# A four-layer cross-attention kernel on one core: the ternary feed-forward stage joined and re-staged, and an opening that waits for two batches only

## The reference

```python
def bitlinear(x, W, b):
    w_scale = jnp.clip(jnp.mean(jnp.abs(W)), EPS, None)
    Wq = _ste(W, jnp.clip(jnp.round(W / w_scale), -1.0, 1.0) * w_scale)
    x_scale = jnp.clip(jnp.max(jnp.abs(x), axis=-1, keepdims=True), EPS, None)
    xq = _ste(x, jnp.clip(jnp.round(x * (QB / x_scale)), -QB - 1.0, QB) * (x_scale / QB))
    return jnp.einsum('bnd,hd->bnh', xq, Wq) + b
h = bitlinear(x, W1, b1)          # 128 -> 512
h = jax.nn.gelu(h, approximate=False)
return bitlinear(h, W2, b2)       # 512 -> 128
```

## Time and profile before

| | |
|---|---|
| time, median of 3 runs | 2486.17 us (2484.84 to 2491.94) |
| the profiled execution: time | 2488.64 us |
| the profiled execution: span of its records | 2486.9 us |
| busy: PE, DVE, ACT, POOL | 2136.2, 1824.4, 1335.7, 1247.5 us |
| mean granted clock of PE | 0.946 of 2.4 GHz |
| opening, to the first record of the attention | 0 to 22.78 us |
| ternary phase, from its first record to the end | 2360.99 to 2486.9 us |

### The profile page before, as it was taken

One profiled execution on the slowest core, in us unless ns is written; L12 is line 12 of the kernel. 1 busy time (PEld: TensorE's weight loads), 2 busy tenths in 40 slices (PEclk: granted clock), 3 DMA queues, 4 the chain that ended last, 5 costly groups with the idle time before them and its releaser, 6 DMA issues. The chain is left out here.

```text
span 2486.9 us, 67321 instructions
## 1 busy us (share of the span) xinstructions
PE 2136.2 (86%) x22352; PEld 1629.6 (66%) x22352; DVE 1824.4 (73%) x4650; ACT 1335.7 (54%) x2821; POOL 1247.5 (50%) x1940
## 2 busy tenths in 40 slices
PE   5878997999988779599999997899789999998755
PEld 4557995556656568466666666666567888875523
DVE  5975554666659766489999968688698866667887
ACT  2444552444434456355555547355468888873466
POOL 4547635555535366477777745333264343334333
PEclk9978998999999879799999999899999999999978
DMA  8022211000000223200000000000000312210000
GB/s 307 20 112 76 78 53 30 16 13 14 11 2 1 83 76 105 62 13 11 9 9 11 8 2 21 10 1 0 19 5 2 103 56 67 56 43 15 1 11 24
DMA packets 82031, 96.69 MB, mean 39 GB/s; under 512 B 16720, under 2 KB 61136, under 8 KB 79760
## 3 DMA queue, kind: packets, MB, share of 16 engines
q1 hardware_dynamic: 73616, 77.12, 9.9%
q0 software_dynamic: 8192, 16.79, 2.3%
HBM read 56.51 MB, written 37.36 MB: 38 GB/s over the span
## 5 line engine op out<-in xcount | busy, mean ns | idle before, releaser
L1722 DVE TENSOR_TENSOR l2f_h_lo<-l2f_h,l2f_h_hi 128x512 fp32r<-128x512 f32 x256 | 187.1, 763 | 101.1 <-ACT l2f_h_hi L1643 101.0
L1012 POOL TENSOR_TENSOR a_pm<-a_pt,tri_post 128x256 f32<-128x256 f32 x256 | 179.6, 731 | 71.8 <-ACT a_pt L668 71.4
L1650 ACT ACTIVATE l2f_h<-l2f_f,ahead 128x512 f32<-128x512 f32 x256 | 174.2, 688 | 49.6 <-DVE l2f_h_lo L1722 32.5
L808 DVE TENSOR_REDUCE l1s_negm<-l1s_s 128x6 bf16<-128x768 f32 x128 | 123.1, 961 | 95.7 <-PE l1s_s L485 95.5
L1817 POOL TENSOR_TENSOR l2f_acc<-l2f_tmp,l2f_acc 128x512 f32<-128x512 f32 x56 | 73.0, 1303 | 207.2 <-DVE l2f_tmp L1740 207.2
L668 ACT ACTIVATE l1s_pt<-l1s_st 128x768 f32<-128x768 f32 x128 | 96.9, 812 | 144.9 <-PE l1s_st L523 144.9
L808 DVE TENSOR_REDUCE a_negm<-a_s 128x4 bf16<-128x1024 f32 x128 | 156.2, 1220 | 23.2 <-PE a_s L485 23.1
L1643 ACT ACTIVATE l2f_h_hi<-l2f_h 128x512 fp32r<-128x512 f32 x256 | 154.4, 633 | 0.0
L668 ACT ACTIVATE a_pt<-a_st 128x1024 f32<-128x1024 f32 x128 | 126.6, 1066 | 3.3 <-PE a_st L523 3.3
L684 ACT ACTIVATE a_q_hi<-a_pa 128x256 bf16<-128x256 f32 x64 | 24.5, 383 | 184.7 <-PE a_pa L451 184.7
L1534 PE MATMUL l2f_f<-l2f_x_hi,l2f_w_hi 128*128 128x512 f32 x256 | 101.7, 397 | 1.2 <-POOL l2f_w_lo L1804 1.2
(11 more groups left out here) (575 smaller groups left out, 6930.1 us busy)
## 6 DMA issues: line engine op xcount, KB each, us to landing
expert_rows<-zeros SPq DMA_DIRECT2D x16, 1056.0 KB, 17.5
l2f_wrow<-weights_by_expert SPq DMA_DIRECT2D x64, 256.0 KB, 3.2
l0f_w<-in_l0f_w SPq DMA_DIRECT2D x8, 640.0 KB, 9.7
l0f_x_in_sb<-expert_rows SPq DMA_DIRECT2D x72, 64.0 KB
expert_rows<-l0f_y SPq DMA_DIRECT2D x72, 64.0 KB, 1.6
l1f_x_in_sb<-expert_rows SPq DMA_DIRECT2D x72, 64.0 KB
expert_rows<-l1f_y SPq DMA_DIRECT2D x72, 64.0 KB
ahead<-in_l2f_w SPq DMA_DIRECT2D x6, 512.0 KB, 4.6
```

Source lines behind the costliest of these rows:

```text
L808: dve.tensor_reduce(dst, src, AX.X, ALU.max, negate=True).then_inc(max_done, 1)
L1012: last = pool.tensor_tensor(pm[:, par, heads_, kt, :], pt[:, par, heads_, kt * (T + P):kt * (T + P) + P], K["tri_post"][:].unsqueeze(1).br ...
L1650: act.activation(h[:, j], psum_f[j][:], ACT.Gelu, bias=col(e, j)).then_inc(h_ready, 1)
L1722: dve.tensor_tensor(h_lo[:, pos % 2, j], h[:, j], h_hi[:, pos % 2, j].bitcast(F32), ALU.subtract)\
```

## The change

**In the opening**, x is loaded in two parts, batches 0 and 1 ahead and the other 14 after the first weights; the end of the phase waits for the first part alone, and DVE waits for the rest (`arrived`) where the attention takes the statistics of batch 2. DVE clears `context_t`, `context_n` and `zeros` before it needs `begin_rstd`, and POOL makes `begin_rstd` after 10 of its 25 masks. ACT runs a one-element activation early.

The diff, cut to its core (line numbers of the changed kernel are some 5 to 35 higher):

```diff
-            sp.dma_start(x[:], a["x"].rearrange("b (t p) d -> p (b t) d", p=P)).then_inc(in_loaded, 16)
+            rows = a["x"].rearrange("b (t p) d -> p (b t) d", p=P)
+            first = slice(0, 2 * TT)
+            rest = slice(2 * TT, NT)
+            sp.dma_start(x[:, first, :], rows[:, first, :]).then_inc(in_loaded, 16)
             sp.dma_start(ctx_t[0:CK, :], a["ctx_t"]).then_inc(in_loaded, 16)
             fetch(sp, K, None, after)
+            sp.dma_start(x[:, rest, :], rows[:, rest, :]).then_inc(K["arrived"], 16)
...
-            dve.wait_ge(step, MASK_STEPS)
-            dve.tensor_reduce(K["own_slot"][:], K["slots4_8"][:].rearrange("p (u q) -> p u q", u=4), AX.X, ALU.add)\
-                .then_inc(filled, 1)
-            dve.wait_ge(filled, 2)
-            dve.wait_ge(rstd_ready, 1)
-            for t in range(CTILES):
-                last = dve.tensor_scalar(cn[:, t, :], c[:, t, :], mv[:, t, 0:1], rstd[:, t:t + 1],
-                                         ALU.subtract, ALU.mult)
-            last.then_inc(cn_ready, 1)
             dve.memset(ctx_t[CK:P, :], 0.0).then_inc(zeroed, 1)
             dve.memset(ctx_n[CK:P, :], 0.0)
             dve.wait_ge(zeroed, 1)
             dve.memset(ctx_t[CK:CK + 1, :], 1.0).then_inc(zeroed, 1)
             dve.memset(zeros[:], 0.0).then_inc(zeroed, 1)
             dve.wait_ge(zeroed, 3)
+            dve.wait_ge(rstd_ready, 1)
+            for t in range(CTILES):
+                last = dve.tensor_scalar(cn[:, t, :], c[:, t, :], mv[:, t, 0:1], rstd[:, t:t + 1],
+                                         ALU.subtract, ALU.mult)
+            last.then_inc(cn_ready, 1)
+            dve.wait_ge(step, MASK_STEPS)
+            dve.tensor_reduce(K["own_slot"][:], K["slots4_8"][:].rearrange("p (u q) -> p u q", u=4), AX.X, ALU.add)\
+                .then_inc(filled, 1)
+            dve.wait_ge(filled, 2)
...
+            pool.wait_ge(stats, 1)
+            pool.tensor_scalar(veps[:], mv[:, :, 1], EPS, None, ALU.add).then_inc(veps_ready, 1)
+            pool.wait_ge(veps_ready, 1)
+            pool.tensor_tensor(rstd[:], veps[:], K["half"][:, 0:CTILES], ALU.pow).then_inc(rstd_ready, 1)
...
+            act.activation(warm[:], g[:], ACT.Identity)
...
+                if clear and isinstance(b, int) and b == 2:
+                    dve.wait_ge(K["arrived"], 16)
...
-                if j == -4 and after_first is not None:
-                    after_first()
+                if j + 4 < len(between):
+                    between[j + 4]()
...
-                link(dve.tensor_scalar(wq[:], ws[:], 1.0 / QB, None, ALU.mult))
                 for i in range(2):
-                    link(dve.tensor_scalar(wf[i][:], wf[i][:], wr[:, i:i + 1], ROUND, ALU.mult, ALU.add))
-                    link(dve.tensor_scalar(wf[i][:], wf[i][:], ROUND, 1.0, ALU.subtract, ALU.min))
-                    link(dve.tensor_scalar(wt[i][:], wf[i][:], -1.0, None, ALU.max))
+                    link(dve.tensor_scalar(wq_by_part[:, i:i + 1], ws[:, 1 - i:2 - i], 1.0 / QB, None, ALU.mult))
+
+            def ternary(i):
+                link(dve.tensor_scalar(wf[i][:], wf[i][:], wr[:, i:i + 1], ROUND, ALU.mult, ALU.add))
+                link(dve.tensor_scalar(wf[i][:], wf[i][:], ROUND, 1.0, ALU.subtract, ALU.min))
+                link(dve.tensor_scalar(wt[i][:], wf[i][:], -1.0, None, ALU.max))
+
+            def first_weights():
+                ternary(0)
                 link(dve.tensor_scalar(b1w[:], b1b[:], wr[:, 0:1], QB, ALU.mult, ALU.mult))
                 dve.sem_inc(w_ready, 1)
...
+            def second_weights():
+                ternary(1)
+                dve.sem_inc(w_ready, 1)
+            def rounded(n, pn, q, pq):
+
+                has_h, has_x = inside(n), inside(q)
+                part = slice(0 if has_h else 1, 2 if has_x else 1)
+                if has_h:
+                    dve.wait_ge(h_ready, G * n + G)
+                    dve.tensor_reduce(most[:, 0, :], h[:, pn % 2], AX.X, ALU.max, apply_absolute_value=True)\
+                       .then_inc(qstep, 1 if has_x else 2)
+                if has_x:
+                    dve.wait_ge(xn_ready, q + 1)
+                    dve.tensor_reduce(most[:, 1, :], xn[:, pq % 2], AX.X, ALU.max, apply_absolute_value=True)\
+                       .then_inc(qstep, 1 if has_h else 2)
+                dve.wait_ge(qstep, QS * q + 2)
+                dve.tensor_scalar(clipped[:, part], most[:, part], EPS, None, ALU.max).then_inc(qstep, 1)
+                dve.wait_ge(qstep, QS * q + 3)
+                wait(dve, diag_ready, q - 1 if has_x else N)
+                dve.reciprocal(inverse[:, pq % 2, part], clipped[:, part]).then_inc(qstep, 1)
+                dve.wait_ge(qstep, QS * q + 4)
+                dve.tensor_scalar(scaling[:, part], inverse[:, pq % 2, part], QB, None, ALU.mult).then_inc(qstep, 1)
+                dve.wait_ge(qstep, QS * q + 5)
+                if has_h:
+                    wait(dve, hq_ready, n)
+                    for t in range(G):
+                        last = dve.tensor_scalar(hi[:, t], h[:, pn % 2, t], scaling[:, 0, t:t + 1], ROUND, ALU.mult, ALU.add)
+                    last.then_inc(hi_ready, 1)
+                if has_x:
+                    wait(dve, xq_ready, q)
+                    for t in range(G):
+                        last = dve.tensor_scalar(xi[:, t], xn[:, pq % 2, t], scaling[:, 1, t:t + 1], ROUND, ALU.mult, ALU.add)
+                    last.then_inc(xi_ready, 1)
+                    wait(dve, h_ready, G * (q - 3))
+                if has_h:
+                    wait(dve, o1_ready, n - 3)
+                rows = part.stop - part.start
+                dve.tensor_tensor(back[:, pq, part], clipped[:, part],
+                                  wq_by_part[:, part].unsqueeze(2).broadcast_to([P, rows, G]), ALU.mult).then_inc(qstep, 1)
...
                     dve.wait_ge(stats, k + 1)
                     dve.sem_inc(K["passed"], 1)
+                n, pn = at(0)
+                q, pq = at(3)
+                if inside(n) or inside(q):
+                    rounded(n, pn, q, pq)
...
+            run(dve, emit, (weight_sums, first_weights, second_weights))
...
         def _(pool):
             def emit(at):
-                q, pq = at(3)
-                if inside(q):
-                    pool.wait_ge(xstep, XS * q + 3)
-                    wait(pool, h_done, G * (q - 3))
-                    pool.sem_inc(K["passed"], 1)
-                    o = [P, G, P]
-                    pool.tensor_tensor(diag[:, pq], K["ident"][:].unsqueeze(1).broadcast_to(o),
-                                       xr[:, pq % 2, :].unsqueeze(2).broadcast_to(o), ALU.mult).then_inc(diag_ready, 1)
                 k, pk = at(4)
                 if inside(k):
                     pool.wait_ge(stats, k + 1)
                     wait(pool, xn_ready, k - 1)
+                    wait(pool, shift_ready, k)
...
-            pe.wait_ge(w_ready, 1)
...
+                    pe.wait_ge(hq_ready, l + 1)
+                    wait(pe, hq_t_ready, l)
                     for t in range(G):
                         for f in range(FB):
+                            last = pe.transpose(psum_t[:, t, f, :], hq[:, t, f * P:(f + 1) * P], K["ident_bf"][:])
+                    last.then_inc(h_turned, 1)
...
+                    pe.wait_ge(hq_t_ready, l + 1)
+                    if isinstance(l, int) and l == 0:
+                        pe.wait_ge(w_ready, 2)
+                    wait(pe, o1_ready, l)
...
+            act.activation(warm[:], K["half"][:, 0:1], ACT.Gelu)
...
-                        act.activation(h[:, pm % 2, t], psum_h[pm % 2][t][:], ACT.Gelu, scale=xd[:, pm, t:t + 1])\
+                        act.activation(h[:, pm % 2, t], psum_h[pm % 2][t][:], ACT.Gelu, scale=back[:, pm, 1, t:t + 1])\
                            .then_inc(h_ready, 1)
+                l, pl = at(-1)
+                if inside(l):
+                    act.wait_ge(h_turned, l + 1)
+                    wait(act, o_done, l - 1)
+                    act.activation(hq_t[:, pl % 2], psum_t[:], ACT.Identity).then_inc(hq_t_ready, 1)
                 n, pn = at(2)
...
+                n, pn = at(0)
+                if inside(n):
+                    act.wait_ge(hi_ready, n + 1)
+                    wait(act, h_turned, n)
+                    act.activation(hq[:], hi[:], ACT.Identity, bias=unround[:]).then_inc(hq_ready, 1)
+                q, pq = at(3)
+                if inside(q):
+                    act.wait_ge(xi_ready, q + 1)
+                    wait(act, x_turned, q - 1)
+                    act.activation(xq[:, pq % 2], xi[:], ACT.Identity, bias=unround[:]).then_inc(xq_ready, 1)
```

119 lines of the change are left out of this document (36 added, 83 removed).

## The result

The changed kernel takes 2462.77 us (median of 4 runs, 2459.79 to 2467.61) against 2486.62 us for the kernel before in the same comparison: ratio 0.9902, 95% interval 0.988 to 0.9925. I had forecast 2471 us, with 2464 to 2478 as the range. The two profiled executions are further apart, 27.1 us in span (2486.9 and 2459.8).

| stretch | before, us | after, us | less | forecast |
|---|---|---|---|---|
| up to the ternary phase | 2360.99 | 2353.31 | 7.7 | 4.3 |
| its lead-in, to the first reduction of h | 19.80 | 17.27 | 2.5 | } 4.3 |
| reductions 0 to 2 | 14.28 | 10.26 | 4.0 | |
| reductions 2 to 12 (ten steps) | 66.55 | 54.53 | 12.0 | 5.6 |
| from reduction 12 to the end | 25.28 | 24.43 | 0.85 | 0.8 |

What follows compares the result with a forecast made beforehand. DVE was taken to bound the steady ternary steps, chains across engines the lead-in, DVE's chain the opening. Opening 4.3, lead-in with first steps 4.3, ten steps 5.6 and end 0.8 sum to 15.0 us: 2471 us, range 2464 to 2478.

Steps and rivals of the forecast that it cites:

- three small instructions: Steady ternary step on DVE: three small instructions go, at 0.20 us each.
- clip: Steady step on DVE: `l3f_hc` no longer meets POOL's sum and takes 0.17 instead of 0.62 us, a gain of 0.45.
- collision moved: Steady step: POOL's 0.61 us diagonal slows the product or codes of h instead of `l3f_xi`; net 0.
- the loop's register work: Steady step: the hardware loop's register work is not hidden, so 6.1 us was taken instead of 6.02.
- None takes over: Steady step: neither ACT (4.8 us a step) nor PE (4.0) becomes the bound in place of DVE.
- the later turns: Steady step: the handover from h's codes through ACT and PE to the second layer is spread over two steps.
- Rival (b): Ternary steps: PE's two waits at its lower clock make 7.5 us a step, total 2489 to 2490; chance 0.04.
- Rival (a): Steady step: PE's new round trip sets 6.6 us, so the steady part gives nothing; total 2477, chance 0.17.
- the root first: Lead-in: POOL does the root ahead of the 0.61 us diagonal; part of the lead-in's and first steps' 4.3 us.
- the weights in parts: Lead-in: the second and third part of the weights (2.0 and 1.45 us) stand in waits of the chain.
- the batch-2 wait: Attention's start: waiting for batch 2's tokens costs nothing, standing 5.7 us behind the first statistics.
- the early table load: Opening: the early activation hides ACT's table load, which was not late before either.

## Why the prediction was wrong

**The steady step is the step that failed.** I wrote: "Against that, the aggregate waits for the statistics at once [...] +0.45 to +0.6". By the rows, from 6.59: three small instructions -0.60, product -0.07, clip -0.45, collision moved 0 (all as forecast, -1.12). The aggregate measured by starts: before, 0.56 us from its start to `l3f_o`'s, of which 0.31 are a wait for its own end (the row below and the earlier trace rows); after, 1.14 from the statistics to the reduction of h, less the 0.40 that the statistics take before the next start anyway, so 0.74. That is +0.18. I had charged the new gaps in full and not credited the old gap of 0.31 that goes. The reduction of xn stands behind that of h with nothing between, -0.09. And 0.08 for the loop's register work was not there. Sum 5.56 against 6.1. The kernel with the late aggregate shows that the gross charge was real; the netting was wrong.

```profile
2417.74 0.24 DVE L2798 BATCH_NORM_AGGREGATE l3f_mv<-l3f_st 128x2 f32<-128x6 f32 x2
```

Over ten steps that is 5.4 us; 1.1 more come from where I cut: the tenth step has neither statistics nor aggregate left (4.42 us instead of 5.56), as both now stand ahead of the reduction of h. That is 12.0 against 5.6, and the largest part of what the forecast missed.

**"None takes over" was true of this order only, and for the wrong reason.** I took the later turns at nothing in the steady part, by ACT's 72% and PE's 61%. Without them the shorter step doesn't come about at all: PE's clock falls. Rival (b), the slower side, had the mechanism right and the place wrong: it is the old order of turns that meets it. That its 7.5 us a step lie near the 7.3 measured is luck, since it had summed them for the new order and given the old one 6.9 at that clock. In the new order the idle stretch is split in two, and the step that did fall to the lower clock (from 2410.23 to about 2414, matmuls of 1.91, granted 0.57) still took 5.6. Against (b) I had said that the clock fell after PE had idled for 3.1 to 3.2 us and that nothing over 2 us would be left; the kernel with the turns in their own step fell after 2.3, the changed one once after 1.73. Rival (a) did not come: DVE waited for PE not once in the ten steps.

**The opening.** The direct part was 4.95, between the bounds 3.5 and 5.3, I took 4.3. Another 2.7 us in the profiled executions arose behind the attention's start, 2.35 of them in the attention and what follows it up to the next stage. I had said that everything between the phases keeps its length; nine traces with the very same opening differ by 3.9 us there, on more than one chip, and by up to 1.9 us on one chip. The timed opening alone gained 7.2 us (4.2 to 10.2), which fits 4.95 as well as 7.7.

**Lead-in and steps 0 to 2.** 6.5 against 4.3, of which 1.9 is the clock that the execution of before happened to have. The lead-in's size was right. Of my reasons, the root first or the weights in parts would nearly have done alone, and the two don't add up; the joined scales gave nothing there. The rest is in steps 0 to 2, 10.26 us where I had 12. The end, the batch-2 wait (no idle of DVE ahead of its statistics) and the early table load went as said.
